# One store of scores per tile in an evenly spaced layout, four buffers for it, and the offset products in other gaps

## The chip, the cores and the metric

The kernel runs on one core of a Trainium2 chip. The metric is the device time of one launch in microseconds (us), the median of several executions. The engines are TensorE (PE), VectorE (DVE), ScalarE (ACT), GpSimd (POOL) and SyncE (SP). SP only issues transfers here; POOL issues transfers too. Each engine works through its own instructions in order and meets the others by semaphores.

## The reference, cut to what matters

A block of a transformer on 8192 tokens (2 sequences of 4096) of width 256:

```
xn = layernorm(x)
q, k, v = xn@wq.T+bq, xn@wk.T+bk, xn@wv.T+bv            # 16 heads of 16
off  = tanh(pw @ gelu(depthwise_conv3(q)) + pw_b) * 6    # 12 positions for each head and token
pos  = clip(token + linspace(-2, 2, 12) + off, 0, 4095)
attn = softmax(q . k(pos) / 4 - rel_scale*|pos - token|) # k, v sampled linearly at pos
s    = (sum attn * v(pos)) @ wo.T + bo
ffn  = top-2 of 8 experts, silu(x@A)*(x@B) @ C, weighted
out  = x + s * silu(ffn(xn))
```

Since positions reach at most 8 tokens to either side, the kernel computes for each token and head the slopes of its scores at 16 neighbouring keys, stores them in DRAM as `S`, and later works the 12 samples out of them.

## The kernel before

The tokens are 64 tiles of 128; four tiles are a step (`GROUP`), so there are 16 steps. `front_block` has a first pass (layer norm, values, router) and a second pass; `mix_block` follows when every engine has reached the end of the front (its first instruction starts at 380.87 us). It runs the experts (71 pairs of slots) on PE beside the sampling and weights on DVE, step by step, and ends with the 64 tiles of attention output, whose bands of weights SP loads (`tile_in`, L1146 and L1152).

**Second front pass, one step n.** PE: `head_scores(n, a)` for a = 0 to 3 (256 small matmuls, L645, into the one tile `pS`), `project(n+2, o)` (k and q two steps ahead, L625, into `pQK`), and `offsets(n-1, h)` for h = 0, 1 (L657, into the one tile `pOff`). ACT: `evacuate_s` copies `pS` to a buffer of `Sx` (L527, two instructions), and must have done so before PE's next `head_scores`; `mask_q` (L515), `evacuate_k` (L498), `evacuate_q` (L505), `gelu(n)` (L535), `bases(n-1)` (L542), `tanh(n-1)` (L548). DVE: `positions(n-2)` (L792 to L797), `convolve(n)` (L765 to L773), `slopes_of_k(n+2)` (L754), then `offset_bias(n-1, h)` (L779), each of which PE's next `offsets` waits for.

**The list of experts' tokens.** In step 1 DVE counts tokens and PE adds the counts up; in step 2 `find_slots` runs on DVE between the two `offset_bias`; POOL scatters three quarters of the list, and the rest is placed by PE: in steps 4, 7, 10 and 13 (`PLACE_AT`) DVE builds one-hots (L878, L881) between the two `offset_bias`, and PE's `place` (L671) multiplies them at the end of the step.

**Scores to DRAM.** In PSUM, partition block 2b+f (32 partitions) holds sub-tile 2s+b of the tile (s = 0, 1) and half f of the head pairs. A row is 376 numbers, 47 keys by 8. The read side wants the row of token r shifted by r keys, so that a fixed window of 16 keys is contiguous: rows are written at a pitch of 376 (`S_ROW`) in blocks of 32 and read at a pitch of 384 (`S_PITCH`). Before, blocks of 32 rows stood 32 x 384 apart, which makes one even pitch for the read of 128 partitions, and the store needs four transfers a tile (one for each b and f). `Sx` has two buffers; `evacuate_s` waits for the store of two tiles before.

**Reading them back.** `slopes_in(it)` gives the loads of one step, two of 128 partitions. SP issues those of step 0 in the front (`load_opening`, after step `OPEN_AT` = 5, with two loads of positions), those of steps 1 to 14 in the mix stage (`reload_slope`, L1114, each followed by the positions, L1115), and POOL the last. Step 1's are issued at the opening of the mix stage behind the expert weights; step 14's stand on SP ahead of the tile loads from tile 4 on. In between `Fori` loops issue store, positions and reload once a step.

**End of the front.** After step 15 PE does `offsets(15, h)`; ACT's `bases(15)` and `tanh(15)` follow, DVE finishes the list (L955 to L957) and `positions(15)`, SP stores the positions, and the mix stage begins.

Of the kernel before, what the change touches and what calls it, by code (L numbers as in the profile page):

```python
# [29 lines left out]
P = 128  # L30
# [41 lines left out]
OPEN_AT = PLACE_AT[0] + 1  # L72
# [33 lines left out]
S_PITCH = S_ROW + HPAIRS  # L106
VROWS = TOKENS + P
# [40 lines left out]
def front_block(nc, io, dram, keep):  # L148


    with ExitStack() as ctx:
# [21 lines left out]
        Sx = stage[:, 4 * GROUP_F - SX_F:].rearrange("p (u s k) -> p u s k", u=2, s=SUBS // 2)  # L173

        slope_mem = keep["slope"][:]
        pos_mem = keep["pos"][:]

# [6 lines left out]
        assert LOW_F + HIGH_F + SX_F <= 4 * GROUP_F  # L184
# [95 lines left out]
        sx_stored = [sem(f"sx_stored{u}") for u in range(2)]  # L280
# [26 lines left out]
        STORES = 16 * 2 * 2  # L307
# [23 lines left out]
        def _(sp):  # L331
# [76 lines left out]
            for u in range(2):  # L408
                sp.wait_ge(xn_stored[u], 16 * (STEPS // 2))
                sp.wait_ge(v_stored[u], 16 * (STEPS // 2))  # L410
                sp.wait_ge(pos_stored[u], 16 * (STEPS // 2))
                sp.wait_ge(sx_stored[u], STORES * (TILES // 2))

# [53 lines left out]
        def _(act):  # L467
# [50 lines left out]
            def evacuate_s(n, a):  # L518
# [5 lines left out]
                if N >= 2:  # L524
                    act.wait_ge(sx_stored[a % 2], STORES * (N // 2))
                for s in range(HALVES):
                    ins = nc.scalar.activation(  # L527
                        Sx[:, a % 2, s].rearrange("p (k c g) -> p k c g", c=KC, g=RG),
                        pS[:, :, 0:KC * HALVES * SKEYS].rearrange("p g (c s k) -> p s k c g", c=KC, s=HALVES)[:, s],
                        ACT.Identity)  # L530
# [36 lines left out]
            for n in range(STEPS):  # L567
# [8 lines left out]
                if more:  # L576
                    evacuate_q(n + 2)
                evacuate_s(n, 2)
                gelu(n)
# [4 lines left out]
                else:  # L584
# [6 lines left out]
        def _(pe):  # L591
# [95 lines left out]
            for n in range(STEPS):  # L687
                head_scores(n, 0)
# [15 lines left out]
            offsets(STEPS - 1, 0)  # L704
            offsets(STEPS - 1, 1)

        @block.vector
        def _(dve):
# [241 lines left out]
            positions(STEPS - 2)  # L950
            for h in range(2):
                offset_bias(STEPS - 1, h)
# [4 lines left out]
            V.scalar_tensor_tensor(keep["inv"][:], pInv[:, 0:HIGH], float(TOKENS), high_row[:], ALU.add, ALU.add)  # L957
            positions(STEPS - 1)


def mix_block(nc, io, dram, keep):
# [4 lines left out]
    with ExitStack() as ctx:  # L966
# [339 lines left out]
        def _(act):  # L1306
# [73 lines left out]
            def prepare(it):  # L1380
# [11 lines left out]
                if it < LAST:  # L1392
                    act.wait_ge(s_loaded, 16 * 2 * it + 16 * 2)
                else:
                    act.wait_ge(end_s_loaded, 16 * 2)
# [196 lines left out]
        def _(dve):  # L1592
# [15 lines left out]
            def bends(it):  # L1608

                if it < LAST:  # L1610
                    dve.wait_ge(s_loaded, 16 * 2 * it + 16 * 2)
                else:
                    dve.wait_ge(end_s_loaded, 16 * 2)
# [155 lines left out]
def build(nc, io):  # L1769
    dram = {  # L1770
        "xn": nc.dram_tensor("xn_rows", [TOKENS + SPARE, XROW], F32).ap(),
        "S": nc.dram_tensor("S_rows", [2, TOKENS, S_PITCH], F32).ap(),
# [7 lines left out]
    with ExitStack() as ctx:  # L1780
# [67 lines left out]
```

## Time and profile before

| | us |
|---|---|
| median of 3 runs (1513.81 to 1520.91) | 1514.63 |
| the profiled execution | 1504.55 |
| its span, first to last instruction | 1502.9 |
| PE busy in the span | 1367.6 (91%) |
| DVE busy | 1291.8 (86%) |
| ACT busy | 825.1 (55%) |
| POOL busy | 771.3 (51%) |

The profile is of one execution, which was shorter than the three of the median; durations are compared with its own time. Busy shares are means over stages with different limits, so the table doesn't say what limits a stage. A wait in the trace is the idle time of an engine in front of an instruction, with the instruction that released it.

### The profile page before, as it was taken

Reading aid. Unit: us, or ns where it says so; the run is one execution under the profiler, and the core shown is the slowest. Engines: PE = TensorE matmul, PEld = TensorE weight load, DVE = VectorE, ACT = ScalarE, POOL = GpSimd, SP = SyncE. Lnnn points to the kernel's source line nnn. Section 1 sums busy time; section 2 is a strip of 40 time slices with the busy share of each in tenths; the row PEclk is TensorE's granted clock in tenths of the full one; section 3 lists DMA queues with packets and bytes.
Section 4 is the critical chain, followed back from the end, with each engine's and each line's share of the span. In section 5 each row is a group of like instructions: output and inputs, shape, how many; then the busy total and the mean of one; then the engine's idle time right before and its main releaser. Section 6 shows DMA issues by size and latency. Waiting matters only on the chain.

```text
span 1502.9 us, 35945 instructions
## 1 busy us (share of the span) xinstructions
PE 1367.6 (91%) x13751; PEld 1093.9 (73%) x13752; DVE 1291.8 (86%) x1544; ACT 825.1 (55%) x1889; POOL 771.3 (51%) x530
## 2 busy tenths in 40 slices
PE   5998898996599999999999899999999878788897
PEld 4864565565488888888888788888888766666675
DVE  7837655654799999999999999999999999999971
ACT  2547666775355645554564445555555446566565
POOL 1001577430667867677666867777576651211021
PEclk9998999997799999999999999999999988899999
DMA  7935576665756776767676575767677679999898
GB/s 229 349 132 99 129 201 173 177 183 152 255 159 180 217 217 177 230 153 229 159 238 181 153 232 149 214 165 220 163 207 198 148 180 225 258 203 254 224 239 160
DMA packets 203994, 293.52 MB, mean 195 GB/s; under 512 B 25345, under 2 KB 160773, under 8 KB 203635
## 3 DMA queue, kind: packets, MB, share of 16 engines
q0 software_dynamic: 64672, 146.57, 37.8%
q1 hardware_dynamic: 136547, 144.84, 34.4%
q8 instruction: 52, 0.85, 0.3%
q10 hardware_dynamic: 2672, 0.83, 0.2%
q14 instruction: 51, 0.42, 0.1%
HBM read 182.83 MB, written 117.73 MB: 200 GB/s over the span
## 4 chain that ended last, share of the span: by engine, by line
DVE 50%; PE 7%; DMA 7%; issue 7%; SPq 3%; ACT 0%; POOL 0%; POOLq 0%; DVEq 0%; ACTq 0%
DVE gslope L1678 12%; DVE parts L1674 12%; DVE parts L1634 8%; DMA band<-band_rows 6%; DVE expert_mem L1600 5%; DVE parts L1646 3%; PE pB L1511 2%; DVE parts L1650 2%; DVE parts L1653 1%; SPq L1152 1%; PE pA L1496 1%; PE pY L1521 1%; SPq L1146 1%; DVE gslope L1731 1%; DVE wgt L1739 1%
## 5 line engine op out<-in xcount | busy, mean ns | idle before, releaser
L1206 POOL DMA_INDIRECT moe_rows<-expert_mem,token_of x142 | 335.0, 2359 | 78.2 <-issue 50.3
L1477 PE MATMUL pA<-xsT,expert_mem 128*128 128x256 f32 x1136 | 265.5, 388 | 17.6 <-DMA expert_mem<-in_w_l 13.9
L1187 POOL DMA_INDIRECT expert_mem<-xn_rows,token_of x142 | 212.0, 1493 | 122.6 <-issue 69.3
L1483 PE MATMUL pY<-expert_mem 128*128 x1136 | 264.2, 386 | 0.0
L1477 PEld LDWEIGHTS pA<-xsT,expert_mem 128*128 128x128 f32 x1136 | 221.4, 195 | 50.6 <-issue 13.8
L1477 PE MATMUL pB<-xsT,expert_mem 128*128 128x256 f32 x1136 | 256.8, 379 | 0.0
L1483 PEld LDWEIGHTS pY<-expert_mem 128*128 128x128 f32 x1136 | 210.0, 190 | 41.8 <-issue 16.1
L1477 PEld LDWEIGHTS pB<-xsT,expert_mem 128*128 128x128 f32 x1136 | 215.8, 190 | 29.3
L1674 DVE SCALAR_TENSOR_TENSOR parts<-pos_pair,prob 128x768 f32<-128x768 f32 x256 | 227.8, 951 | 1.1
L1678 DVE TENSOR_REDUCE gslope<-parts 128x256 f32<-128x3072 f32 x64 | 214.7, 3354 | 2.2
L1328 ACT ACTIVATE expert_mem<-pA,b1sel 128x256 f32<-128x256 f32 x284 | 111.3, 475 | 136.5 <-issue 95.9
L1634 DVE SCALAR_TENSOR_TENSOR parts<-posT,bend 128x768 f32<-128x768 f32 x192 | 168.9, 948 | 1.0 <-ACT posT L1389 1.0
L1337 ACT ACTIVATE expert_mem<-pB,b1sel 128x256 f32<-128x256 f32 x284 | 111.5, 476 | 93.7 <-PE pB L1477 93.7
L1346 ACT ACTIVATE expert_mem<-pY,gsel 128x256 f32<-128x256 f32 x142 | 59.6, 471 | 157.0 <-PE pY L1483 157.0
L450 POOL DMA_INDIRECT slot_list<-token_i,high_part x96 | 102.8, 1070 | 47.2 <-issue 29.0
L625 PE MATMUL pQK<-qT,wqk 128*128 128x512 f32 x256 | 122.0, 621 | 1.5 <-ACT qT L505 0.8
L1196 POOL DMA_DIRECT2D expert_mem<-in_w_l x71 | 66.8, 942 | 100.4 <-PE pX L1471 64.4
L1245 POOL DMA_DIRECT2D out<-expert_mem x15 | 19.4, 1296 | 188.2 <-DVE expert_mem L1685 171.2
L1600 DVE TENSOR_TENSOR expert_mem<-expert_mem 128x1024 f32<-128x1024 f32 x71 | 87.1, 1226 | 8.2 <-ACT expert_mem L1337 4.6
L1646 DVE TENSOR_TENSOR parts<-parts 128x5376 f32<-128x5376 f32 x16 | 92.3, 5767 | 0.5
L645 PEld LDWEIGHTS pS<-kT,qm 32*64 32x64 f32 x4096 | 55.1, 139 | 48.9 <-issue 44.2
L645 PE MATMUL pS<-kT,qm 32*64 32x47 f32 x4096 | 64.0, 245 | 26.5 <-ACT stage L527 22.3
(207 smaller groups left out, 2047.0 us busy)
## 6 DMA issues: line engine op xcount, KB each, us to landing
expert_mem<-in_w_l POOLq DMA_DIRECT2D x71, 1024.0 KB, 7.0
band<-band_rows SPq DMA_DIRECT2D x256, 96.0 KB, 5.4
S_rows<-stage SPq DMA_DIRECT2D x256, 94.0 KB
band_rows<-wgt SPq DMA_DIRECT2D x12, 1536.0 KB, 7.3
pos_pair<-pos_rows SPq DMA_DIRECT2D x28, 384.0 KB, 8.1
xn_rows<-stage SPq DMA_DIRECT2D x16, 512.0 KB, 5.3
v_rows<-stage SPq DMA_DIRECT2D x16, 512.0 KB, 4.2
moe_rows<-zeros POOLq DMA_DIRECT2D x4, 2048.0 KB
```

The lines of the kernel that those rows point to most:

```text
L625: mm = nc.tensor.matmul(pQK[:, c], wqk[:, k, first:first + P], qT[:, k, qcol(m):qcol(m) + GTOK], start=(k == 0), stop=(k == KC - 1))
L645: mm = nc.tensor.matmul(pS[s % 2 * 2 * SUB:(s % 2 + 1) * 2 * SUB, g, col:col + SKEYS], qm[rows, a // 2, c, a % 2 * SUBS + s].rearrange("p ...
L1187: nc.gpsimd.indirect_dma_start(out=xs[:, u, s], out_offset=None, in_=dram["xn"], in_offset=bass.IndirectOffsetOnAxis(ap=keep["inv"][:, 2 * ...
L1206: nc.gpsimd.indirect_dma_start(out=dram["moe"], out_offset=bass.IndirectOffsetOnAxis(ap=keep["inv"][:, 2 * n + s:2 * n + s + 1], axis=0), ...
L1337: ins = nc.scalar.activation(hid[:, h, c], pB[:, c], ACT.Identity, bias=b1sel[:, u, HC + c:HC + c + 1])
L1477: mm = nc.tensor.matmul(dst[:, c], w1[:, 1 - u, k, o * HID + c * P:o * HID + (c + 1) * P], xsT[:, k], start=(k == 0), stop=(k == KC - 1))
L1483: mm = nc.tensor.matmul(pY[:, s], hid[:, h, c, s * P:(s + 1) * P], w2[:, c, ds(e * D, D)], start=False, stop=(s == 1 and c == HC - 1))
L1600: V.tensor_tensor(hid[:, h], hid[:, h], act_a[:, h % 2], ALU.mult).then_inc(hid_ready, 1)
L1634: ins = V.scalar_tensor_tensor(in_block(parts[:, i]), in_block(posT[:].rearrange("p b q -> p (b q)")), float(i + 1 - REACH), each_in_block ...
L1646: chain.count(V.tensor_tensor(parts[:, 0:7], parts[:, 0:7], parts[:, 7:14], ALU.add))
L1674: ins = V.scalar_tensor_tensor(terms[:, i], at, float(j - REACH), prob[:], ALU.max, ALU.mult)
L1678: chain(V.tensor_reduce(G[:, :, batch * BATCHED:(batch + 1) * BATCHED].rearrange("p t j -> p j t"), terms.rearrange("p j (t r) -> p j t r" ...
```

## The change

One store for each tile: the 128 partitions of `Sx` go to DRAM as blocks of 32 x 376 numbers without gaps, so partitions and halves are evenly spaced. The read therefore has an even pitch only within 32 partitions: `slopes_in` gives eight loads of 32 partitions in place of two of 128, and the waits on `s_loaded` and `end_s_loaded` count 16 x 8 for a step. `Sx` has four buffers, one for each tile of a step. They take the room of the one-hots `is_low` and `at_high`, which move to the memory of `slope` and `pos_pair`; so `load_opening`, which fills those, moves from step 5 to step 14 and waits for the last `place`. On PE the offsets of the step before move from the gaps before and after `head_scores(n, 2)` to those after `head_scores(n, 2)` and after `head_scores(n, 3)`. In the last two steps, which have no `project`, they take the gaps of the projects, and the offsets of step 15 the two gaps behind. ACT's `gelu(15)` comes before `evacuate_s(15, 2)`, `bases(14)` and `tanh(14)` before `evacuate_s(15, 3)`. DVE finishes the list ahead of the last `offset_bias` and of `positions(14)`.

```diff
-OPEN_AT = PLACE_AT[0] + 1
+OPEN_AT = PLACE_AT[-1] + 1
+S_BLOCK = SUB * S_ROW
+S_TILE = 2 * SUBS * S_BLOCK
+SX_SLOTS = 4
...
-        is_low = stage[:, 0:LOW_F].rearrange("p (i n) -> p i n", i=ONE_HOT)
-        at_high = stage[:, LOW_F:LOW_F + HIGH_F].rearrange("p (i n) -> p i n", i=ONE_HOT)
-        SX_F = 2 * (SUBS // 2) * S_ROW
+        SX_F = SX_SLOTS * (SUBS // 2) * S_ROW
+        is_low = slope_mem[:, 0:LOW_F].rearrange("p (i n) -> p i n", i=ONE_HOT)
+        at_high = pos_mem[:, 0:HIGH_F].rearrange("p (i n) -> p i n", i=ONE_HOT)
...
             def store_s(n, a):
                 sp.wait_ge(s_ready, n * GROUP + a + 1)
-                tok = n * GTOK + a * P
-                for b in range(2):
-                    for f in range(2):
-                        rows = slice((2 * b + f) * SUB, (2 * b + f + 1) * SUB)
-                        sp.dma_start(
-                            bass.AP(dram["S"].tensor, (tok + b * SUB) * S_PITCH + f * TOKENS * S_PITCH,
-                                    [[S_ROW, SUB], [2 * SUB * S_PITCH, HALVES], [1, S_ROW]]),
-                            Sx[rows, a % 2]).then_inc(sx_stored[a % 2], 16)
+                sp.dma_start(bass.AP(dram["S"].tensor, (n * GROUP + a) * S_TILE, [[S_ROW, P], [4 * S_BLOCK, HALVES], [1, S_ROW]]),
+                             Sx[:, a]).then_inc(sx_stored[a], 16)
...
-                sp.wait_ge(list_rows, 1)
-                for u in range(2):
-                    sp.wait_ge(sx_stored[u], STORES * (GROUP // 2))
+                sp.wait_ge(placed, CHUNKS)
+                for u in range(SX_SLOTS):
+                    sp.wait_ge(sx_stored[u], 16)
...
-                if N >= 2:
-                    act.wait_ge(sx_stored[a % 2], STORES * (N // 2))
+                if n > 0:
+                    act.wait_ge(sx_stored[a], 16 * n)
...
+                if n == STEPS - 1:
+                    gelu(n)
                 evacuate_s(n, 2)
-                gelu(n)
+                if n < STEPS - 1:
+                    gelu(n)
+                else:
+                    bases(n - 1)
+                    tanh(n - 1)
                 evacuate_s(n, 3)
...
                 head_scores(n, 0)
-                if n + 2 < STEPS:
+                if more:
                     project(n + 2, 0)
+                else:
+                    offsets(n - 1, 0)
                 head_scores(n, 1)
-                if n + 2 < STEPS:
+                if more:
                     project(n + 2, 1)
-                if n > 0:
+                else:
+                    offsets(n - 1, 1)
+                head_scores(n, 2)
+                if more and n > 0:
                     offsets(n - 1, 0)
-                head_scores(n, 2)
-                if n > 0:
+                if n == STEPS - 1:
+                    offsets(n, 0)
+                head_scores(n, 3)
+                if more and n > 0:
                     offsets(n - 1, 1)
-                head_scores(n, 3)
+                if n == STEPS - 1:
+                    offsets(n, 1)
...
-            positions(STEPS - 2)
-            for h in range(2):
-                offset_bias(STEPS - 1, h)
             dve.wait_ge(placed, CHUNKS)
             dve.wait_ge(list_loaded, 16)
...
+            offset_bias(STEPS - 1, 0)
+            positions(STEPS - 2)
+            offset_bias(STEPS - 1, 1)
             positions(STEPS - 1)
...
         def slopes_in(it):
-            return [(keep["slope"][:].rearrange("p (a f jh) -> p f a jh", a=GROUP, f=2)[:, f],
-                     bass.AP(dram["S"].tensor, (f * TOKENS + it * GTOK) * S_PITCH,
-                             [[S_PITCH, P], [P * S_PITCH, GROUP], [1, KNOTS * HPAIRS]])) for f in range(2)]
+            return [(keep["slope"][q * SUB:(q + 1) * SUB].rearrange("p (a f jh) -> p f a jh", a=GROUP, f=2)[:, f],
+                     bass.AP(dram["S"].tensor, it * GROUP * S_TILE + (q * 2 + f) * S_BLOCK,
+                             [[S_PITCH, SUB], [S_TILE, GROUP], [1, KNOTS * HPAIRS]])) for q in range(SUBS) for f in range(2)]
```

## Rows read from the trace of the kernel before

**Rows 1.** The page, part 4: the chain that ended last, by engine.

```profile
DVE 50%; PE 7%; DMA 7%; issue 7%; SPq 3%; ACT 0%; POOL 0%; POOLq 0%; DVEq 0%; ACTq 0%
```

**Rows 2.** Busy time in stretches: us, engines, PEclk, DMA share, GB/s.

```profile
110.00:338.00 228.00, 203.37 (x4076) 131.30 (x4076) 141.52 (x274) 160.07 (x302) 115.09 (x108) 0.97 0.61 158
338.00:381.00 43.00, 23.21 (x571) 20.14 (x570) 19.57 (x43) 21.81 (x47) 0.00 (x0) 0.72 0.53 143
381.00:1207.00 826.00, 802.25 (x3716) 680.85 (x3717) 810.59 (x686) 427.76 (x1079) 592.04 (x352) 0.98 0.69 193
1207.00:1378.00 171.00, 139.58 (x2670) 107.57 (x2668) 166.31 (x142) 97.64 (x213) 41.05 (x33) 0.87 0.99 229
```

**Rows 3.** Waits from 110 to 381 us: total us, times, longest.

```profile
PE pS L645 <- ACT stage L527: 22.3, 16, 3.1
ACT stage L527 <- DMA S_rows<-stage: 19.1, 11, 4.7
```

**Rows 4.** Timeline of PE in step 7: start, duration, instruction, [idle before it].

```profile
232.68 3.70 PE L625 MATMUL pQK<-qT,wqk 128*128 128x512 f32 x8
236.22 1.46 PE L657 MATMUL pOff<-pw_w,conv 128*128 128x192 f32 x8
...
241.67 2.21 PE L671 MATMUL pInv<-stage 128*128 128x142 f32 x16 [0.54 <-DVE stage L881]
245.31 0.93 PE L645 MATMUL pS<-kT,qm 32*64 32x47 f32 x60 [1.43 <-ACT stage L527]
```

**Rows 5.** Timeline of ACT: the GELU of step 3 and that of step 13.

```profile
173.03 1.06 ACT L535 ACTIVATE conv<-conv 128x1024 f32<-128x1024 f32 x1
...
334.82 1.06 ACT L535 ACTIVATE conv<-conv 128x1024 f32<-128x1024 f32 x1
```

**Rows 6.** Issues of SP by line: ns min/median/max, first and last start us.

```profile
L352 SPq DMA_DIRECT2D S_rows<-stage x256: 315/431/2321, 112.2 to 367.7; - x128
...
L1114 SPq DMA_DIRECT2D slope<-S_rows x28: 368/528/4876, 402.7 to 1222.0; - x28
```

**Rows 7.** Groups of ACT from 190 to 420 us: busy us, mean ns.

```profile
L527 ACT ACTIVATE stage<-pS 128x376 f32<-128x376 f32 x90 | 38.6, 481 | 39.0 <-PE pS L645 19.5 <-DMA S_rows<-stage 19.1
...
L542 ACT ACTIVATE pos<-anchor,base 128x192 f32<-128x192 f32 x52 | 19.3, 450 | 0.0
...
L505 ACT ACTIVATE qT<-pQK,bqk_col 128x512 f32<-128x512 f32 x18 | 11.4, 684 | 13.4 <-PE pQK L625 13.4
...
L548 ACT ACTIVATE off<-off 128x768 f32<-128x768 f32 x13 | 10.8, 833 | 4.8 <-DVE off L779 4.8
```

**Rows 8.** Timeline: tanh behind the list (step 2), and one-hots of step 7.

```profile
163.00 0.84 ACT L548 ACTIVATE off<-off 128x768 f32<-128x768 f32 x1 [2.01 <-DVE off L779]
...
239.33 2.28 DVE L881 TENSOR_SCALAR stage<-high_row,slot_high,token 128x142 f32<-128x142 f32 x8
```

**Rows 9.** Timeline of the last two steps.

```profile
341.57 1.05 PE L645 MATMUL pS<-kT,qm 32*64 32x47 f32 x64 [2.24 <-ACT stage L527]
...
359.77 1.41 DVE L773 SCALAR_TENSOR_TENSOR conv<-qT,dw_w,conv 128x512 f32<-128x512 f32 x2
...
370.96 2.90 PE L657 MATMUL pOff<-pw_w,conv 128*128 128x192 f32 x8 [4.14 <-DVE off L779]
...
375.37 0.96 DVE L792 SCALAR_TENSOR_TENSOR pos<-off,pos 128x768 f32<-128x768 f32 x1
...
376.66 1.01 DVE L797 TENSOR_SCALAR pos<-pos,base 128x192 f32<-128x192 f32 x4
```

**Rows 10.** Timeline and chain at the opening of the mix stage.

```profile
402.71 4.48 SPq L1114 DMA_DIRECT2D slope<-S_rows  x2
...
407.24 8.44 DMA pos_pair<-pos_rows
...
415.70 1.63 ACT L1389 ACTIVATE posT<-pos_pair,shift 128x192 f32<-128x192 f32 x4 [2.45 <-DMA pos_pair<-pos_rows]
```

**Rows 11.** Timeline of SP at the beginning of the end stage.

```profile
1221.62 1.90 SPq L1114 DMA_DIRECT2D slope<-S_rows  x2
```

More of the change, by code:

```diff
@@ L169, in front_block @@
         v = stage[:, 2 * GROUP_F:].rearrange("p (u a c) -> p u a c", u=2, a=GROUP)
-        is_low = stage[:, 0:LOW_F].rearrange("p (i n) -> p i n", i=ONE_HOT)
-        at_high = stage[:, LOW_F:LOW_F + HIGH_F].rearrange("p (i n) -> p i n", i=ONE_HOT)
-        SX_F = 2 * (SUBS // 2) * S_ROW
-        Sx = stage[:, 4 * GROUP_F - SX_F:].rearrange("p (u s k) -> p u s k", u=2, s=SUBS // 2)
+        SX_F = SX_SLOTS * (SUBS // 2) * S_ROW
+        Sx = stage[:, 4 * GROUP_F - SX_F:].rearrange("p (u s k) -> p u s k", u=SX_SLOTS, s=SUBS // 2)
         slope_mem = keep["slope"][:]
         pos_mem = keep["pos"][:]
+        is_low = slope_mem[:, 0:LOW_F].rearrange("p (i n) -> p i n", i=ONE_HOT)
+        at_high = pos_mem[:, 0:HIGH_F].rearrange("p (i n) -> p i n", i=ONE_HOT)
         def per_token(mem, i):
@@ L183, in front_block @@
         chosen = [per_token(stage, k) for k in range(TOPK)]
-        assert LOW_F + HIGH_F + SX_F <= 4 * GROUP_F
+        assert LOW_F <= GROUP_F and HIGH_F <= 2 * PAIRS and TOPK * TE_F + SX_F <= 4 * GROUP_F
         wqk = sb("wqk", [P, KC, 2 * D])
@@ L279, in front_block @@
         s_ready = sem("s_ready")
-        sx_stored = [sem(f"sx_stored{u}") for u in range(2)]
+        sx_stored = [sem(f"sx_stored{u}") for u in range(SX_SLOTS)]
         conv_chain = sem("conv_chain")
@@ L306, in front_block @@
         HALVES = SUBS // 2
-        STORES = 16 * 2 * 2
         WEIGHTS = 16 * 7
@@ L411, in _ @@
                 sp.wait_ge(pos_stored[u], 16 * (STEPS // 2))
-                sp.wait_ge(sx_stored[u], STORES * (TILES // 2))
+            for u in range(SX_SLOTS):
+                sp.wait_ge(sx_stored[u], 16 * STEPS)
         @block.gpsimd
@@ L583, in _ @@
                     nc.scalar.activation(expw, prod, ACT.Exp).then_inc(exp_out, 1)
-                else:
+                elif n < STEPS - 1:
                     bases(n - 1)
@@ L687, in _ @@
             for n in range(STEPS):
+                more = n + 2 < STEPS
                 head_scores(n, 0)
-                if n + 2 < STEPS:
+                if more:
                     project(n + 2, 0)
+                else:
+                    offsets(n - 1, 0)
                 head_scores(n, 1)
-                if n + 2 < STEPS:
+                if more:
                     project(n + 2, 1)
-                if n > 0:
+                else:
+                    offsets(n - 1, 1)
+                head_scores(n, 2)
+                if more and n > 0:
                     offsets(n - 1, 0)
-                head_scores(n, 2)
-                if n > 0:
+                if n == STEPS - 1:
+                    offsets(n, 0)
+                head_scores(n, 3)
+                if more and n > 0:
                     offsets(n - 1, 1)
-                head_scores(n, 3)
+                if n == STEPS - 1:
+                    offsets(n, 1)
                 if n == COUNT_AT:
@@ L703, in _ @@
                     place(PLACE_AT.index(n))
-            offsets(STEPS - 1, 0)
-            offsets(STEPS - 1, 1)
         @block.vector
@@ L1392, in prepare @@
                 if it < LAST:
-                    act.wait_ge(s_loaded, 16 * 2 * it + 16 * 2)
+                    act.wait_ge(s_loaded, 16 * 2 * SUBS * it + 16 * 2 * SUBS)
                 else:
-                    act.wait_ge(end_s_loaded, 16 * 2)
+                    act.wait_ge(end_s_loaded, 16 * 2 * SUBS)
                 for dst, first in ((base, 0), (last4, KNOTS - BLOCKS)):
@@ L1610, in bends @@
                 if it < LAST:
-                    dve.wait_ge(s_loaded, 16 * 2 * it + 16 * 2)
+                    dve.wait_ge(s_loaded, 16 * 2 * SUBS * it + 16 * 2 * SUBS)
                 else:
-                    dve.wait_ge(end_s_loaded, 16 * 2)
+                    dve.wait_ge(end_s_loaded, 16 * 2 * SUBS)
                 bend_v = bend[:].rearrange("p j (g h) -> p g j h", h=HPAIRS)
@@ L1771, in build @@
         "xn": nc.dram_tensor("xn_rows", [TOKENS + SPARE, XROW], F32).ap(),
-        "S": nc.dram_tensor("S_rows", [2, TOKENS, S_PITCH], F32).ap(),
+        "S": nc.dram_tensor("S_rows", [TILES, S_TILE], F32).ap(),
         "v": nc.dram_tensor("v_rows", [VROWS, D], F32).ap(),
```

2 lines of the change are left out of this document (1 added, 1 removed).

## The prediction

> **What bounds the kernel now.** I read the page first: VectorE (DVE) has half of the chain that ended last [rows 1]. Busy time by stretch then splits the run [rows 2]: from 381 to 1207 us DVE is 98% busy (810.6 of 826 us), and nothing of its work there is touched. The change acts on the second front pass, about 110 to 381 us, a serial prologue: what it saves starts everything later so much earlier. There the busiest engine is TensorE (PE), 203.4 of 228 us up to 338 us, and 23.2 of 43 us, at a mean granted clock of 0.72, in the last stretch. So the pass is an in-order PE queue with holes. The waits name the holes [rows 3]: PE waited 22.3 us for the copies of the scores by ScalarE (ACT), and ACT waited 19.1 us for earlier stores of scores. The two overlap and can't be added.
>
> **Work of one step.** The timeline of step 7 gives PE's pitch [rows 4]: a project 3.54 us, the score group behind it about 0.9, and 5.45 from the first offsets to `place` (two offsets, two score groups), of which 0.54 is a wait: 4.91. Two projects and two more score groups make 13.8 us; `place` adds 2.2. The ten steps from the GELU of step 3 to that of step 13 now take 161.8 us [rows 5], 16.2 each, though only three of them (4, 7, 10) hold a `place`.
>
> **One store, four buffers.** 256 stores become 64, so 192 issues of 0.431 us (83 us of SP's queue) go [rows 6]; SP waits most of the time there, so this alone is worth nothing. What counts is that a buffer is reused four tiles later, a whole step, not two: the 11 waits of ACT (19.1 us, the longest 4.7 [rows 3]) should all go.
>
> **Offsets in other gaps.** Old order on PE: scores 0, project, scores 1, project, offsets 0, scores 2, offsets 1, scores 3, and straight on to the next scores 0, which must wait for ACT's copy of scores 3 (1.43 us in step 7 [rows 4]). New: the offsets stand behind scores 2 and behind scores 3. I check the new gaps from durations [rows 7]. After the second project, ACT still has two q copies (2 x 0.684) and the two halves of the score copy (0.86) ahead of scores 3: 2.2 us plus some 0.3 of signalling, against 0.95 + 1.46 of scores 2 and offsets 0 on PE. It just fits. Behind scores 3, offsets 1 cover the copy. Tanh and its bias come some 2 us later, but the next step begins with a 3.5 us project, so ACT catches up. A step without `place` should run at PE's own 13.8.
> A step with `place` gains less: DVE needs 3.9 us from the end of offsets 0 (237.68 [rows 4]) to the last one-hot (239.33 + 2.28 = 241.61 [rows 8]), and PE now has only scores 3 and offsets 1 to fill it, 2.4 us against 3.4. PE waits 1.6, not 0.54: 13.8 + 1.6 + 2.1 = 17.5.
> Seven steps at 13.8 and three at 17.5 are 149.1, so 12.7 us less than 161.8. Against it: in step 2 `find_slots` stands on DVE between the two offset biases, and ACT's tanh waits for the second [rows 8]. The count of step 1 and this list now both begin one score group (0.9) later, about 2 us together. Net 10.7.
>
> **One-hots and opening loads.** The one-hots move to other memory with the same shapes: nothing. The opening loads leave step 5 for step 14 and wait there for the last `place`, done by then. Their ten issues take SP about 4.5 us; four buffers cover ACT meanwhile. They have over 15 us to land before the mix stage begins, and the nearest row, a load of positions in heavy traffic, took 8.44 [rows 10]. Taken as nothing; if late, each us is paid in full, up to about 5.
>
> **Last two steps.** Now the scores of step 14 begin at 341.57 and the last `positions` ends at 377.67 [rows 9], 36.1 us later. New, counting from that start: the convolution of step 15 ends at about 19.7, as now (361.18), since it hangs on tanh 13 and DVE's order in both. Then the first bias of 14 to 20.3, offsets 14 to 21.9, scores 2 and the first offsets of 15 to 24.4; meanwhile ACT's copy, bases (1.8 issued, 1.5 net) and tanh 14 (0.83) to 26.2; positions 14 (2.0) to 28.3, a bias and tanh 15 to 29.8, positions 15 (2.3) to 32.2. PE stays sparse, and one group of offsets in this stretch took 2.90 us [rows 9] against 1.46 [rows 4], half the clock; two such on the chain give 35. I take 33.5, 2.6 less. Step 14 also starts 0.4 earlier, since the 4.7 us wait before it [rows 3], most of it under `place`, is gone. Together 3.
>
> **Loads of scores cut in eight.** The price of the new layout: a step's two loads (128 partitions) become eight (32 partitions), 32 in all become 128, the bytes unchanged. In the middle it is free: a reload is issued about a step (67 us) ahead. Two places are not covered.
> At the opening of the mix stage, SP issues two loads from 402.71 to 407.19 and then the positions, for which ACT waits 2.45 us; DVE's products wait for ACT [rows 10]. Six more issues at 0.43 are 2.6 us if they add in full; nothing, if the backlog of transfers sets the landing, as 8.44 us for that one suggest. I take 1.
> At 1221.62 the last reload on SP stands ahead of the tile loads [rows 11], which PE waits for. Six more issues are 2.6 us, or less what these two take above 0.43 each (1.6); the DMA share is 0.99 there [rows 2], which hides some. I take 1.5. POOL's single reload, near 1285, gains six issues, needed some 60 us later: nothing.
> The Trainium skill (DMA: Bandwidth & Descriptors, Rules for kernel authors) advises one 128-partition transfer over transfers for parts of the partitions: it speaks for the store and against these loads. No row here shows its size.
>
> **Sum.** 10.7 + 3 - 1 - 1.5 = 11.2 us less. The profiled execution took 1504.55 us (span 1502.9, 1.65 around it), so 1493.4. The median shown, 1514.63, is of other executions, 10 us longer; I carry the difference over: 1503.5 us.
>
> **Rivals.**
> - Gain nearly twice mine: the copies fit with time to spare, steps run at 13.4, the last two steps take 32.2, the loads cost nothing: 10.7 + 2.8 + 4.3, 18 and a little for a higher clock, 20. Then 1494.6. Against it: DVE's and ACT's latencies in the last steps don't depend on PE.
> - The waits move and are not removed: scores 3 wait for ACT's q copies in every step. The fit above has no margin, so 0.5 us or more a step is easily lost, 5 to 8 in all. About 1510 us, within 0.5%.
> - Slower, by the eight loads. With transfers queued, two issues took 4.48 us [rows 10], the second 3.9 of them, and the longest single one 4.876 [rows 6]. If such a price comes with each load and not with its bytes, six more at the opening are 23 us, and six at 1221.62 at 0.95 each (1.90 for two [rows 11]) 5.7: 14 gained, 29 lost, 1530 us. It decides from 1.15 us for each of the twelve. Against it: the median issue is 0.528 [rows 6], with 128 partitions a piece.
> - The same skill page (Anatomy of one DMA) fits a fixed part of about 2.0 us to each transfer of GpSimd; twelve in sequence would be 24 us, an estimate by that page alone.
> - Only the order helps and the buffers do nothing: the pitch is 13.8 in most steps and some 3 us of stalls stay. Inside my range.
>
> **Chances.** Forecast (7.6 to 16 less) 0.45, the larger gain 0.15, no gain that can be told 0.29, slower 0.11. A measurement of this kernel tells a change from none at about 0.5%, 7.6 us. So faster 0.60, same 0.29, slower 0.11. Range 1494 (the larger gain) to 1516 (the gain lost and the loads at their upper bounds); about 0.2 lies outside.
>
> **What would show it.** No ACT wait for the stores of scores; GELU to GELU 13.8 in steps without `place`, about 17.5 with; a PE wait of 1.6 before `place`; the first instruction of the mix stage 12 to 15 us before 380.9; ACT's wait for positions at its opening 1 to 3 us longer; the stretch from the last reload to the end as long as now within 3 us. The prediction is wrong if steps stay near 15 with scores 3 waiting for ACT, if the last two steps take over 36 us, or if the mix stage grows by more than 5.

## The result, and the profile after

The changed kernel took 1504.01 us (median of 5 runs, 1500.45 to 1505.08), the kernel before 1515.33 us beside it (5 runs, 1513.81 to 1520.91): a ratio of 0.9913, interval 0.9889 to 0.9937. It is 11.3 us faster by the medians, and the interval of the ratio reaches from 9.5 to 16.8 us; predicted were 1503.5 us and 11.2 us. The sum is right; its terms are less so, and the two profiled executions alone would have hidden the gain. Their times are 1504.55 us before and 1504.18 after (spans 1502.9 and 1502.5), because the profiled execution of before happened to lie 10 us below its own median. So the stretches are compared, not the spans.

Busy time of each engine in four stretches of the kernel after (start and end, length, then PE, PEld, DVE, ACT, POOL, granted clock, DMA share, GB/s), in answer to [rows 2]:

```profile
110.00:338.00 228.00, 209.69 (x4161) 133.06 (x4160) 145.38 (x282) 163.55 (x312) 116.92 (x108) 0.97 0.49 159
338.00:381.00 43.00, 19.02 (x494) 16.00 (x492) 25.47 (x48) 22.65 (x49) 7.67 (x6) 0.68 0.52 172
381.00:1207.00 826.00, 808.04 (x3741) 683.71 (x3742) 807.49 (x680) 423.74 (x1072) 593.25 (x349) 0.99 0.71 193
176.60:190.20 13.60, 13.60 (x290) 8.54 (x289) 8.22 (x15) 11.20 (x23) 10.86 (x10) 1.00 0.43 146
```

PE is busier in the pass (209.7 us against 203.4), and in the fourth row, one step without `place`, it is busy for all of its 13.60 us: the queue has no hole left in that step. DVE is as full as before in the middle, which the change leaves alone.

The waits of the kernel after in the second pass, 110 to 381 us (engine and line, what it waited for, us in total, times, longest), in answer to [rows 3]:

```profile
PE pInv L675 <- DVE pos_pair L892: 6.2, 4, 1.7
PE pS L649 <- ACT stage L525: 5.8, 4, 2.4
```

PE's wait for ACT's score copies fell from 22.3 us to 5.8, and ACT's wait for the stores (19.1 us) is in the list no more. None of the four waits for copies lies between the GELUs of steps 3 and 13. The first row is the price: PE now waits 6.2 us in all before the four `place`, where it waited 2.5.

PE in step 7 of the kernel after (start, length, form, count, wait ahead of it), in answer to [rows 4]:

```profile
231.72 3.70 PE L629 MATMUL pQK<-qT,wqk 128*128 128x512 f32 x8
235.35 0.88 PE L649 MATMUL pS<-kT,qm 32*64 32x47 f32 x64
236.16 1.57 PE L661 MATMUL pOff<-pw_w,conv 128*128 128x192 f32 x8
237.66 0.88 PE L649 MATMUL pS<-kT,qm 32*64 32x47 f32 x64
238.47 1.57 PE L661 MATMUL pOff<-pw_w,conv 128*128 128x192 f32 x8
241.71 2.21 PE L675 MATMUL pInv<-pos_pair,slope 128*128 128x142 f32 x16 [1.67 <-DVE pos_pair L892]
```

Scores 3 and the second offsets run back to back, and then `place` finds the one-hots not yet there: 1.67 us, where 1.6 was forecast. The GELUs that bound steps 3 to 13, in answer to [rows 5]:

```profile
176.58 1.07 ACT L533 ACTIVATE conv<-conv 128x1024 f32<-128x1024 f32 x1
...
329.47 1.07 ACT L533 ACTIVATE conv<-conv 128x1024 f32<-128x1024 f32 x1
```

Ten steps take 152.89 us, 8.9 less than before; 12.7 less were forecast. The last two steps, in answer to [rows 9]:

```profile
335.89 0.89 PE L649 MATMUL pS<-kT,qm 32*64 32x47 f32 x64
...
354.00 1.41 DVE L784 SCALAR_TENSOR_TENSOR conv<-qT,dw_w,conv 128x512 f32<-128x512 f32 x2
...
367.34 1.00 DVE L808 TENSOR_SCALAR pos<-pos,base 128x192 f32<-128x192 f32 x4
```

From the first scores of step 14 to the last of `positions` is 32.5 us, against 36.1 before and 33.5 forecast. Then the opening of the mix stage, SP's issues and those that wait for them, in answer to [rows 10]:

```profile
394.57 6.88 SPq L1125 DMA_DIRECT2D slope<-S_rows  x8
401.49 0.73 SPq L1126 DMA_DIRECT2D pos_pair<-pos_rows  x1
408.26 1.16 DVE L1626 TENSOR_TENSOR bend<-slope 128x960 f32<-128x960 f32 x1 [3.45 <-DMA slope<-S_rows]
409.96 1.63 ACT L1400 ACTIVATE posT<-pos_pair,shift 128x192 f32<-128x192 f32 x4 [6.67 <-DMA pos_pair<-pos_rows]
411.69 10.52 DVE L1645 SCALAR_TENSOR_TENSOR parts<-posT,bend 128x768 f32<-128x768 f32 x12 [1.40 <-ACT posT L1400]
```

The chain that ended last has its own row for the load of positions:

```profile
401.49 8.44 DMA pos_pair<-pos_rows
```

It lands 8.44 us after its issue, to the hundredth as before, which is chance: over all profiles ACT has the positions 7.4 to 12.3 us after their issue. So what the issues take is added in full. The eight take 6.9 us with the gaps (0.86 each) where the two took 4.5, and ACT waits 6.67 us where it waited 2.45. That is 2.4 us; another 1.0 lies ahead of them, for SP comes to its first load of scores 22.9 us after the start of the mix stage, not 21.8.

**The landmarks.** The span of every profile is cut at five events: the first scores of the second pass, SP's first issue of the mix stage, and DVE's weights (`wgt`) of mix steps 0, 11 and 14. The lengths between them are differences of start times in the timeline, in us. "Pass" has all that was meant to gain, "opening" and "end stage" the two places where the eight loads were not covered.

| profile of | score loads | pass | opening | middle | end stage | rest |
|---|---|---|---|---|---|---|
| before | 2 | 270.8 | 98.7 | 738.8 | 195.3 | 89.2 |
| before_again | 2 | 271.2 | 99.5 | 739.1 | 198.2 | 89.2 |
| eight_loads | 8 | 276.2 | 103.6 | 739.2 | 200.6 | 90.8 |
| order_only | 2 | 269.4 | 101.6 | 739.3 | 204.1 | 90.4 |
| store_only | 8 | 264.3 | 103.0 | 739.2 | 195.2 | 91.0 |
| after | 8 | 259.7 | 102.1 | 739.0 | 199.7 | 90.0 |
| after_again | 8 | 263.8 | 107.2 | 739.1 | 201.7 | 89.0 |
| old_layout | 2 | 258.0 | 98.7 | 739.2 | 197.8 | 88.5 |
| no_tail | 8 | 259.9 | 103.7 | 739.2 | 202.0 | 90.7 |
| mixed_order | 2 | 253.8 | 98.8 | 739.0 | 200.6 | 89.1 |
| mixed_order_again | 2 | 254.1 | 100.1 | 738.8 | 206.7 | 90.5 |
| mixed_new | 8 | 251.7 | 100.3 | 739.0 | 198.3 | 91.0 |
| mixed_new_early | 8 | 254.3 | 100.8 | 738.9 | 199.0 | 90.3 |

Between the profiles of before and after the pass loses 11.1 us, the opening gains 3.4, the end stage 4.3 and the rest 0.8, and the first pass happens to be 2.0 longer: 0.4 in all. The end stage is 195 to 207 us in kernels that differ there by the cut of one reload at most, and 200.6 and 206.7 in two profiles of one kernel (mixed_order), so a single profile says nothing of it to 3 us.

### The profile page after: what moved, and what is told of

Read it like the earlier page. It is cut to its first block, busy times and chain, and to the rows that moved or that the text cites. A ratio compares the mean times of both kernels' runs of the same rounds, so it can differ in the third digit from the quotient of the medians.

```text
span 1502.5 us, 35981 instructions
## 1 busy us (share of the span) xinstructions
PE 1371.1 (91%) x13751; PEld 1092.3 (73%) x13752; DVE 1292.2 (86%) x1544; ACT 823.2 (55%) x1889; POOL 782.2 (52%) x536
## 3 DMA queue, kind: packets, MB, share of 16 engines
q0 software_dynamic: 64768, 146.57, 38.4%
## 4 chain that ended last, share of the span: by engine, by line
DVE 50%; PE 8%; issue 7%; DMA 6%; SPq 3%; ACT 1%; POOL 0%; POOLq 0%; DVEq 0%; ACTq 0%
DVE gslope L1689 12%; DVE parts L1685 12%; DVE parts L1645 8%; DMA band<-band_rows 5%; DVE expert_mem L1611 5%; PE pB L1522 3%; DVE parts L1657 2%; DVE parts L1661 2%; DVE parts L1664 1%; PE pY L1532 1%; PE pA L1507 1%; DVE gslope L1742 1%; DVE wgt L1750 1%; SPq L1163 1%; PE pBT L1507 1%
## 5 line engine op out<-in xcount | busy, mean ns | idle before, releaser
L1217 POOL DMA_INDIRECT moe_rows<-expert_mem,token_of x142 | 342.7, 2413 | 78.5 <-issue 44.5
L1198 POOL DMA_INDIRECT expert_mem<-xn_rows,token_of x142 | 210.2, 1480 | 139.4 <-issue 90.3
L1488 PE MATMUL pA<-xsT,expert_mem 128*128 128x256 f32 x1136 | 263.8, 386 | 15.3 <-DMA expert_mem<-in_w_l 11.4
L1207 POOL DMA_DIRECT2D expert_mem<-in_w_l x71 | 70.7, 996 | 76.3 <-PE pX L1482 45.2
L629 PEld LDWEIGHTS pQK<-qT,wqk 128*128 128x128 f32 x256 | 47.5, 195 | 53.4 <-issue 49.4
```

The source lines that it names most:

```text
L629: mm = nc.tensor.matmul(pQK[:, c], wqk[:, k, first:first + P], qT[:, k, qcol(m):qcol(m) + GTOK], start=(k == 0), stop=(k == KC - 1))
L1198: nc.gpsimd.indirect_dma_start(out=xs[:, u, s], out_offset=None, in_=dram["xn"], in_offset=bass.IndirectOffsetOnAxis(ap=keep["inv"][:, 2 * ...
L1217: nc.gpsimd.indirect_dma_start(out=dram["moe"], out_offset=bass.IndirectOffsetOnAxis(ap=keep["inv"][:, 2 * n + s:2 * n + s + 1], axis=0), ...
L1488: mm = nc.tensor.matmul(dst[:, c], w1[:, 1 - u, k, o * HID + c * P:o * HID + (c + 1) * P], xsT[:, k], start=(k == 0), stop=(k == KC - 1))
```

## The experiments

Of each timed kernel the ratio to the kernel before is given, run beside it on the same chip. It is not formed from the medians and can differ from their ratio by 2 us in 1500.

**The kernel before, a second time.** No edit.

> The kernel before, unchanged, for a second profile. The profiled execution of before took 1504.55 us, its timed ones 1513.8 to 1520.9; the one after 1504.18, inside its own 1500.45 to 1505.08. Theory A (the profiled execution of before was a lucky one): this profile comes out near 1514, and its surplus of about 10 us lies in the mix stage or in the first pass, where the change touches nothing; the second front pass takes 270.8 us again, the time from the mix stage's first instruction to the end of weights of step 0 98.7 us, within 1. Theory B (the second front pass varies by itself): the surplus lies in the second front pass, and the 11.1 us by which it became shorter in the profile after are partly chance. Ratio 1.000 in both, within 0.003.

1514.37 us, 1.0004 (0.9981 to 1.0028). Its profiled execution took 1508.41, 4 us more than the first one, of which 2.9 lie in the end stage; the pass took 271.2 us against 270.8. Its waits in the second pass:

```profile
PE pS L645 <- ACT stage L527: 20.1, 16, 2.6
ACT stage L527 <- DMA S_rows<-stage: 13.9, 10, 4.9
```

The pattern of [rows 3] is the kernel's; its size varies by 5 us from one execution to another.

**Order alone.** The kernel before, two buffers and all, with PE's, ACT's and DVE's new order (that of the last two steps too, not shown).

```diff
+                head_scores(n, 2)
                 if more and n > 0:
                     offsets(n - 1, 0)
-                head_scores(n, 2)
...
+                head_scores(n, 3)
                 if more and n > 0:
                     offsets(n - 1, 1)
-                head_scores(n, 3)
```

> The kernel before with its layout, two buffers and two loads, and only the new order of offsets, GELU, tanh and list. Theory A (the order gives most of it and the buffers the rest): the second front pass goes from 270.8 to about 263 us; ACT still waits for stores, now with nothing behind to hide it, 10 to 20 us in all; 6 to 9 us faster, ratio 0.994 to 0.996. Theory B (the order needs the buffers, since PE's queue has no slack left for a late score copy): the pass gains under 3 us. Theory C (the buffers do nothing): it gains the whole 11 us.

1514.52 us, 1.0005 (0.9985 to 1.0024): nothing that can be told. Its waits, and one place where they strike:

```profile
ACT stage L527 <- DMA S_rows<-stage: 21.8, 7, 5.6
PE pS L651 <- ACT stage L527: 11.2, 7, 3.8
```

```profile
212.90 0.86 ACT L527 ACTIVATE stage<-pS 128x376 f32<-128x376 f32 x2 [4.93 <-DMA S_rows<-stage]
...
213.90 1.20 PE L651 MATMUL pS<-kT,qm 32*64 32x47 f32 x64 [3.85 <-ACT stage L527]
215.03 5.19 PE L631 MATMUL pQK<-qT,wqk 128*128 128x512 f32 x8
```

ACT waits 4.93 us for a store out of its buffer, PE behind it 3.85, and the project after the hole takes 5.19 us instead of 3.70 (over 215 to 221 us the granted clock averages 0.74). The order fills PE's queue so tightly that a late store goes straight into the pitch; two steps are 20.1 and 21.0 us long.

**Buffers and layout alone.** The changed kernel with the order of before.

> The changed kernel (one store, four buffers, new layout, eight loads, opening after step 14) with the old order of offsets, GELU, tanh and list. Theory A (each half of the change needs the other: with four buffers the store waits go, but PE still waits once a step for ACT's copy): steps without place 14.4 to 15, with place 16.5 to 17, step 3's GELU to step 13's about 153 to 156 us, the end of the pass as before (46 less 2), 3 to 7 us faster than before in all, ratio 0.995 to 0.998. Theory B (the four buffers are the whole gain and the order gives nothing, as alone): 0.991 to 0.993, like the changed kernel. Theory C (buffers alone are worth nothing, since place hides the waits): 1.000.

1507.06 us, 0.9951 (0.9935 to 0.9967): 7.4 us of the gain by the ratio, 8.3 by the medians. No wait for stores is left, but the holes behind the score copies are:

```profile
PE pS L643 <- ACT stage L525: 14.5, 13, 2.0
```

The timed intervals of this kernel and of the changed one touch, so the times alone hardly show what the order adds. The ten steps from the GELU of step 3 to that of step 13 do. With two buffers and the old order they take 161.8, 164.0 and 168.4 us (the last in eight_loads, below), with the order alone 157.9, with the buffers alone 157.5, and with both 152.9 and 152.7 in the changed kernel, 151.8 in old_layout and 152.7 in no_tail. What the order alone saves there it loses again behind: from the GELU of step 13 to the mix stage it takes 47.7 us, against 46.1 and 44.7 in the kernel before.

**Four stores, two loads.** The changed kernel in the old layout, which takes the single store and the eight loads away and keeps order and buffers.

```diff
-                sp.dma_start(bass.AP(dram["S"].tensor, (n * GROUP + a) * S_TILE, [[S_ROW, P], [4 * S_BLOCK, HALVES], [1, S_ROW]]),
-                             Sx[:, a]).then_inc(sx_stored[a], 16)
+                        sp.dma_start(
+                            bass.AP(dram["S"].tensor, (tok + b * SUB) * S_PITCH + f * TOKENS * S_PITCH,
+                                    [[S_ROW, SUB], [2 * SUB * S_PITCH, HALVES], [1, S_ROW]]),
+                            Sx[rows, a]).then_inc(sx_stored[a], 16)
```

> The changed kernel with four buffers and the new order, but the old layout: four stores a tile, two loads of 128 partitions a step. Theory A (the single store only saves SP's idle time and its layout costs at the opening): the second front pass as after, 259.7 us within 1, the opening back at about 99 us until the end of weights of step 0, not 102.1; 3 to 6 us faster than the changed kernel, ratio to before 0.987 to 0.990. Theory B (the single store matters, since ACT would wait again for four stores a tile): the front is 2 us or more longer than 259.7 and the whole no faster than the changed kernel, 0.991.

1502.31 us, 0.9922 (0.9897 to 0.9946), and a pass of 258.0: as fast as the changed kernel. The opening is back at 98.7, as was expected, but the 3 to 6 us by which this kernel was to be faster aren't in the times. The new layout as a whole, one store and eight loads, is worth nothing that can be told; and the single store isn't what rid ACT of its waits, since four stores with four buffers leave none either.

**Eight loads alone.** The kernel before, its two loads of scores cut in eight.

```diff
-            return [(keep["slope"][:].rearrange("p (a f jh) -> p f a jh", a=GROUP, f=2)[:, f],
+            return [(keep["slope"][q * SUB:(q + 1) * SUB].rearrange("p (a f jh) -> p f a jh", a=GROUP, f=2)[:, f],
...
-                              [[S_PITCH, P], [P * S_PITCH, GROUP], [1, KNOTS * HPAIRS]])) for f in range(2)]
+                              [[S_PITCH, SUB], [P * S_PITCH, GROUP], [1, KNOTS * HPAIRS]])) for q in range(SUBS) for f in range(2)]
```

> The kernel before with its old layout, and only the loads of scores cut from two of 128 partitions to eight of 32. Theory A (cut loads cost issue time at the two uncovered places): the opening of the mix stage grows by 3 to 4 us (98.7 to about 102 us until the end of weights of step 0), the wait of DVE for the slopes appears, the end stage grows by 0 to 5; the whole is 3 to 8 us slower, ratio 1.002 to 1.005. Theory B (the longer opening after the change has another cause, such as PE's colder start or the earlier opening loads): no change, ratio 1.000, opening at 98.7. Theory C (each cut load pays for itself): 20 us or more slower.

1514.83 us, 0.9989 (0.9969 to 1.001), while its profile shows the cost at the opening again, on SP and on DVE:

```profile
411.79 6.85 SPq L1114 DMA_DIRECT2D slope<-S_rows  x8
```

```profile
DVE bend L1615 <- DMA slope<-S_rows: 3.9, 1, 3.9
```

Over the table the opening is 103.3 us in the mean of the six profiles with eight loads (mixed_new_early, below, apart) and 99.5 of the six with two: 3.8 us. From its first load of scores to the positions SP takes 6.8 us in the mean of the first six and 4.2 in that of the other: 2.6 us, which is six times 0.43. The rest is not issue time of the loads: SP comes to them 0.7 us later, and ACT has the positions 9.5 us after their issue, not 9.0; with single profiles from 7.4 to 12.3, that may be chance. The end stage is 199.6 against 200.5: no cost to be seen. But the interval of this timed pair reaches only to 1.5 us slower. The profiles show where 3.8 us are lost, the times don't show them lost; that stays open.

**The changed kernel, a second time.** No edit.

> The changed kernel, unchanged, for a second profile. Expected: the second front pass 259.7 us within 1, since nothing in it waits for a transfer any more (the two profiles of before gave 270.8 and 271.2, one of them with other step lengths); the opening of the mix stage 102 to 104 us until the end of weights of step 0, if the eight loads cost there (the kernels with two loads gave 98.7, 99.5, 98.7 and, once, 101.6), and 99 to 100 if the first profile was chance. Ratio 0.991 within 0.002.

1503.0 us, 0.9924 (0.9894 to 0.9954). Its pass was expected within 1 us of the first and is 4.1 longer, 263.8. Of that 3.2 us lie between the first GELU and that of step 3. (Its opening is 107.2 us, above the 102 to 104 expected: ACT waits 11.4 us for the positions there.) The stretch 160 to 178 us, first in the profile of the changed kernel, then in this one:

```profile
160.00:178.00 18.00, 14.96 (x355) 9.66 (x355) 16.25 (x40) 11.93 (x23) 8.00 (x8) 1.00 0.34 117
...
169.25 1.05 PE L649 MATMUL pS<-kT,qm 32*64 32x47 f32 x64 [2.38 <-ACT stage L525]
```

```profile
160.00:178.00 18.00, 15.38 (x224) 8.82 (x222) 14.71 (x35) 10.02 (x22) 8.94 (x9) 0.81 0.29 100
168.00:174.00 6.00, 5.76 (x69) 3.16 (x70) 5.85 (x13) 4.21 (x8) 4.78 (x5) 0.50 0.53 177
...
168.01 1.47 PE L649 MATMUL pS<-kT,qm 32*64 32x47 f32 x64 [2.38 <-ACT stage L525]
169.71 6.11 PE L629 MATMUL pQK<-qT,wqk 128*128 128x512 f32 x8 [0.24 <-ACT kT L496]
```

The granted clock is 1.00 in the one and 0.81 in the other; PE is as long busy and does 224 matmuls instead of 355. Between 168 and 174 us it is 0.50, which is 1.2 GHz, and a project takes 6.11 us instead of 3.70. Ahead of it PE had waited 2.38 us for a score copy; in the first profile it waited the same 2.38 us at the same place, and the clock stayed at 1.00. The same program differs here by more than the orders do.

**The last two steps as before.** The changed kernel with the old sequence in steps 14 and 15, on PE, ACT and DVE.

```diff
                 if more:
                     project(n + 2, 0)
-                else:
-                    offsets(n - 1, 0)
...
+            offsets(STEPS - 1, 0)
+            offsets(STEPS - 1, 1)
```

> The changed kernel with the old sequence in the last two steps only (offsets 14 before and after scores 2 of step 15, both offsets of step 15 at the end, bases and tanh 14 after the last score copy, list after the last biases). Theory A: up to the GELU of step 13 as the changed kernel; from there to the mix stage's first instruction 45 us in place of 42.2, so 3 us slower than the changed kernel, ratio to before about 0.993. Theory B (DVE's and ACT's latencies set it in both): 42 to 43 us, no difference.

Its pass is 259.9 us, and from the GELU of step 13 to the mix stage it takes 42.7 us, against 42.3 in the kernel after and 43.4 in its repetition. So the profiles give the new sequence 0.4 us or nothing. The buffers aren't the reason either, by the stretch from the first scores of step 14 to the mix stage: it takes 39.3, 37.7 and 38.4 us with the old order and two buffers, 38.5 in store_only, and 36.3 in no_tail, 35.8 and 36.9 in the changed kernel. (What the buffers save behind the GELU of step 13 lies ahead of these scores, 4.4 us instead of 6.8.) It became shorter with the new order in the steps before; how is not shown. Timed it took 1507.49 us, 0.9944 (0.9924 to 0.9964), 4.5 us more than the changed kernel beside it (1503.0), but the intervals overlap. Whether the sequence is worth nothing or 3 us isn't settled.

**Both orders, each where it fits.** The `place` wait of 1.6 us and the list's delay in steps 1 and 2 have one cause: the first offsets stand late on PE just where DVE has list work to do. In those steps they go back ahead of scores 2; the other steps keep the new order. Layout of before, four buffers.

```diff
+                list_step = n <= COUNT_AT + 1 or n in PLACE_AT
+                if more and n > 0 and list_step:
+                    offsets(n - 1, 0)
                 head_scores(n, 2)
-                if more and n > 0:
+                if more and n > 0 and not list_step:
                     offsets(n - 1, 0)
```

> Four buffers and the old layout (four stores, two loads), the new order of offsets except in the steps where DVE has list work between its two offset biases (1, 2, 4, 7, 10, 13): there the first offsets stand before scores 2 again, the second behind scores 3. Theory A (the new order starts that list work one score group too late): PE's wait before each place falls from 1.6 to about 0.6 us, steps with place from 17.5 to 16.6, and the first three steps lose 1 us less; 4 to 5 us less than the same kernel with the new order in all steps (its second front pass 258.0), pass about 253.5, ratio to before 0.987 to 0.990. Theory B (scores 3 then wait for ACT, which copies scores 2 later): no gain, 0.992.

> The best kernel so far once more (four buffers, old layout, mixed order), beside the two that follow. Expected: ratio to before 0.987 within 0.003, second front pass 253.8 us within 1.5, opening of the mix stage 98.7 to 99.5 until the end of weights of step 0.

1494.05 us, 0.9872 (0.9845 to 0.9899), and a second time 1494.48, 0.9858 (0.9834 to 0.9883). The pass is 253.8 and 254.1. PE in step 7, where `place` no longer waits. In its stead scores 3 wait 1.04 us for the copy of scores 2, for nothing stands between the two in such a step:

```profile
229.59 1.46 PE L667 MATMUL pOff<-pw_w,conv 128*128 128x192 f32 x8
230.98 0.89 PE L655 MATMUL pS<-kT,qm 32*64 32x47 f32 x64
232.91 0.88 PE L655 MATMUL pS<-kT,qm 32*64 32x47 f32 x64 [1.04 <-ACT stage L531]
233.71 1.57 PE L667 MATMUL pOff<-pw_w,conv 128*128 128x192 f32 x8
235.12 2.13 PE L681 MATMUL pInv<-pos_pair,slope 128*128 128x142 f32 x16
```

Steps with `place` take 15.5 to 15.8 us from GELU to GELU instead of 17.5, but that overstates it: the GELU that begins such a step stands behind scores 2 and so comes one group of offsets later, and the steps before are that much longer. Taken in pairs (GELU 3 to 5, 6 to 8 and 9 to 11) they are 93.7 us against 95.7: 0.6 for each `place`, which is the wait of 1.6 less the 1.04 that comes for it. The first three steps take 49.7 us instead of 52.2, since the list begins earlier again. In all the pass is 5.9 us shorter than in the kernel after, by 2.5 up to GELU 3, 1.7 from there to GELU 13 and 1.7 behind (most of which is only that the GELU of step 13, a step with `place`, comes one group of offsets later). With the two loads at the opening (3.4 us) that would be 9.3 us, and timed it is 9 to 10; but the next kernel has the eight loads and is timed the same, so that sum doesn't explain the times. Like with like, it is 8.3 us below old_layout by the medians, while the pass is 4.2 shorter. This version beats both kernels: the one before by 19 us by the ratio and 21 by the medians, the changed one by 9 to 10.

**The same in the new layout.**

> The same order, with the layout of the change: one store a tile, eight loads a step. The profiles so far show the opening of the mix stage longer with eight loads (102.1 to 107.2 us, five kernels) than with two (98.7 to 101.6, five kernels), but the timed ratios of the pairs with and without them don't differ. Theory A (the opening's 4 to 5 us are real and reach the end): this kernel is 4 to 6 us slower than the one before in this list. Theory B (they are given back, for the end stage is bound by transfers and its start takes up the difference): within 2 us of it, with the opening at 103 again.

1495.52 us, 0.9874 (0.9849 to 0.9899), 1.0 us more than mixed_order beside it, within the scatter. Its opening is 100.3 us, not the 103 expected. In these times too the 3.8 us of the eight loads can't be made out.

**And the first reload earlier.** The reload of step 1 ahead of the four loads of expert weights on SP.

```diff
+            reload_slope(1)
...
-            for it in range(1, 3):
-                reload_slope(it)
+            reload_slope(2)
```

> As the last, with step 1's eight loads and its positions issued before the four large expert weights at the opening of the mix stage, not behind them. Theory A (they queue behind the weights, and each of the eight issues delays the positions): ACT's wait for the positions and DVE's for the slopes go, the opening falls from about 103 to 97 or 98 us, and the kernel is as fast as the two-load one or 1 us faster. Theory B (the cost is in the expert weights, which PE needs in its third period and which now land later): opening no shorter, PE waits for the second weights instead.

1494.3 us, 0.986 (0.9834 to 0.9886). ACT and DVE no longer wait for scores or positions; PE waits for the weights behind them instead, 8.2 us where it waited 2.7 in mixed_new:

```profile
PE pA L1491 <- DMA expert_mem<-in_w_l: 8.2, 2, 5.5
```

The opening is 100.8 us, within the scatter of the rest. What is moved ahead in SP's queue makes the next one late.

## Why the prediction was right, point by point

The mechanism was right: the waits for stores and most waits for copies went, and the pass became shorter. That the sum came out to 0.1 us is luck. The pass lost 11.1 us between the first two profiles where 13.7 were forecast (7.4 by the two repetitions), and the opening gained 3.4 where 1 was forecast. That makes 7.7 us without the end stage, and 11.3 were timed, with an interval from 9.5 to 16.8. What the timed gain has beyond the stretches is open.

- **Four buffers**: right. All of ACT's waits for stores went, in every kernel with four buffers.
- **One store for each tile is worth nothing by itself**: nothing speaks against it. In old_layout the four stores come back together with the two loads, and neither the pass nor the time is longer.
- **Order and buffers as two separate gains**: not put so in the prediction, but its sum prices the order (13.8 a step) and takes the buffers as what makes it hold. The runs bear that out more sharply: timed, order alone 0, buffers alone 7.4 us, both 11 to 13; in the ten steps of the profiles about 4, 4 and 9 against the first profile of before. The rival "only the order helps and the buffers do nothing" fell, the other way round.
- **13.8 us for a step without `place`**: a little low. The seven in steps 3 to 13 took 13.64, 14.76, 14.86, 14.56, 14.37, 14.40 and 13.52, in the mean 14.30. This is the term that was mis-sized: 0.5 us in seven steps is 3.5 of the 3.8 us missing from the 12.7. It was low in PE's own work, not in waits, for PE is busy 98% of these steps. From start to start a project takes 3.63 us before scores and 3.54 only before offsets, as in the row on which the price rested; a group of scores takes 0.81 in one step and 1.05 in another, and with an odd gap of 0.5 to 0.65 us in it, whose cause the profile doesn't show, up to 1.7.
- **17.5 us for a step with `place`, with a wait of 1.6**: right, 17.50, 17.53 and 17.75.
- **The list begins later, 2 us**: right, 1.6 between GELU 0 and 3.
- **The last two steps, 3 us**: the size is near. By their own stretch it is 3.6 (36.1 and 34.5 us in the two profiles of before, 32.5 and 33.6 in those of after), from GELU 13 to the mix stage 3.8, or 2.4 by the second profile of before. The reason is not shown: no_tail has nearly the same length without the sequence on which the sum rested.
- **Opening loads late in the pass**: nothing, as taken, though their ten issues took SP 7.6 us, not 4.5.
- **Opening of the mix stage, 1 us**: mis-sized. The prediction had "2.6 us if they add in full" as the upper bound and chose 1, because the backlog might set the landing. The issues add in full, and 0.43 each was right: 2.4 us between these two profiles, 2.6 over all twelve. So the upper bound was the term. The 3.4 and 3.8 us by which the opening grew hold 1.0 and 1.2 more, of which no run shows that the loads make them.
- **End stage, 1.5 us**: can't be told from nothing among 195 to 207 us.
- **"The first instruction of the mix stage 12 to 15 us before 380.9"**: it came at 371.7, 9.2 before; against the start of the second pass 11.1. Below the forecast, for the mis-sized steps.
- **The rival of nearly twice the gain** fell: steps take 14.3 us, not 13.4, and the opening loads cost something.
- **The rival by which each load has a price of its own** (from 1.15 us each of twelve): six more at the opening cost 2.4 us, 0.4 each. It fell, and the estimate of 24 us for twelve with it. By the Trainium skill (DMA: Bandwidth & Descriptors, Rules for kernel authors) one transfer over 128 partitions is to be preferred to transfers for parts: the opening agrees in sign, 2.6 us of SP's queue for six parts more, and four parts or one for the store, with the loads the other way round, show no difference in time (0.9922 and 0.9913). In these runs it counts only where somebody waits for the queue.
- **The rival "the waits move to scores 3"**: the waits for score copies came to 5.8 us in four places, none of them in the ten steps, not 0.5 a step. It fell.

What is left open: where the opening's 3.8 us go in the timed runs, what the timed gain has beyond the stretches, whether the sequence of the last two steps counts, and what makes the end stage vary.

## What to carry to other kernels

Packing an in-order queue tighter and giving it buffers are one change: here the order alone gained nothing in the timed runs, because PE's tight queue took late stores in full, and the buffers alone left a third or more of the gain behind. Where an instruction feeds two engines by turns, one fixed order need not be right in every step; look which steps have extra work behind it, and order those by themselves: here that was worth another 8 us timed, of which the pass shows 4 to 8 in the profiles. And cut the profile at events of your own and compare each stretch with repeated profiles of the same kernel before a difference of 3 us is given a cause.

## What was not expected of the hardware

- In the first steps of the second pass the granted clock differs between executions of the same program: over 160 to 178 us it is 1.00 in one, and in the other 0.50 (1.2 GHz) from 168 to 174 us, behind the same wait of 2.38 us. The eight matmuls of a project take 3.70 us at the one and up to 6.11 at the other. From GELU 0 to GELU 3 that makes 52.2 or 55.4 us. mixed_new had the clock at 1.00 over 141 to 160 us, where the kernel after has 0.82, and took 46.7.
- The part bound by DVE is steady: 738.8 to 739.3 us in thirteen profiles. The part with heavy transfers behind it spreads over 11 us.
- An issue of one of the eight loads took SP between 0.43 and 1.83 us in the same queue; the positions behind such loads were there 7.4 to 12.3 us after their issue.
